# A four-block image kernel on one core: 34 rows in the upper halves of the quads, a tile's weights copied ahead of the hats, the root's table loaded ahead of the evictions of x

## The chip, the cores and the metric

The kernel runs on one core of a Trainium2 chip. The metric is the device time in microseconds; lower is better. The engines are TensorE (PE, with PEld for its weight loads), VectorE (DVE), ScalarE (ACT), GpSimd (POOL) and SyncE, which issues transfers (SP).

## The reference

Four blocks work one after the other on x of shape (2, 32, 64, 64), each as x = x + block(normalised x), where the normalisation is per channel over the pixels of an image:

```python
x = x + _L0_conv_ref(_gn(x), ...)   # deformable 3x3 conv with a mask, batch norm, relu
x = x + _L1_conv_ref(_gn(x), ...)   # 1x1 conv with sign(x) - tanh(x) + tanh(x)
x = x + _L2_conv_ref(_gn(x), ...)   # deformable 3x3 conv: offsets come from a 3x3 conv of x
x = x + _L3_conv_ref(_gn(x), ...)   # attention over the 4096 pixels of an image
```

A deformable convolution first computes, by a plain 3x3 convolution, two offsets for each of nine taps of each pixel; then it samples the image at the shifted positions with bilinear weights (four corners per tap) and convolves the samples.

## The kernel before

Everything is float32 and lives in SBUF. **Quads.** For L0 and again for L2 the normalised image is written four times, as `quads`, once per corner q of the bilinear square, each on its own 32 partitions and shifted by a row or a column, into a grid of rows with a pitch of 66 elements. One write, `quad_write`, handles one corner q, one image b and one half h of the rows, `HALVES`: rows 0 to 32 (33 rows of 64) and rows 33 to 63 (31 rows). Its source is a run of x; its destination is rows of 64 elements at the pitch of 66. VectorE does ten of the sixteen writes (`some_quads`, line 372), ScalarE six (`other_quads`, line 371). TensorE's convolution for the offsets of a half (`offsets_half`, line 1666) waits on the semaphore `quads_ready[b][h]`, for the four corners of the half and of the half above it.

**L0** then turns the offsets (line 1683), makes row weights and samples with matrix products. **L1** ends with its sums in PSUM; VectorE takes their statistics (line 1068), ScalarE copies them to x (`take_sums`, line 1331), and `deviation` (line 1324) takes the square root of the variance on ScalarE, after which VectorE makes scale and bias and both engines write the quads of L2.

**L2.** TensorE's order is written out by hand: the offsets of image 0, their turning (line 1774), the transposes of the quads of image 0 into rows (`rows`, line 1785), the offsets of image 1 and the turned bands, again turning and rows. ScalarE evicts each. VectorE goes from the quads to `corners(0)` (from line 668), `indices(0)`, `place_bands` (ends at line 951, `bands_made`), `corners(1)`, `indices(1)`. SyncE stores the rows to HBM as `quad_table` (line 453), writes the bands' data to HBM once `bands_made` is there (line 459), and reads them back spread over the partitions (line 477): three groups of three taps are asked for in order, the second after the store of the rows of image 1, the third only after three hats.

GpSimd gathers from `quad_table`, nine gathers (one per tap, line 554) for each tile of 128 pixels, into four slots; 53 tiles in all, 21 of image 0 and 32 of image 1. The gather of a tile waits until the tile four before it has been sampled. VectorE weights the corners of a tile (lines 904, 881), adds them (891, 895), TensorE turns the result (1795), ScalarE evicts it and copies the weights of the next tile to PSUM (`tile`, lines 1432 and 1427), TensorE convolves (1803) and VectorE adds to x (919).

The last 11 tiles of image 0 don't use gathers: `dense_and_tiles` runs 27 steps (three stretches of nine taps, of width 384 and then 512) of products with band matrices. In step n VectorE selects bands for step n+1 (`select_bands`, line 966, from the hats across in PSUM), TensorE mixes bands (`mix_bands`, line 1831), VectorE weighs them (line 978) with the hats down, TensorE convolves (line 1841). ScalarE makes the hats: `hats_of_bands(x, y)` makes those across of step x (lines 1456, 1467) and those down of step y (1462, 1471). Tiles of image 0 are worked between the steps, the first beside step 1. Ahead of the steps ScalarE loads a table, makes the hats of steps 0 and 1, waits until both images are indexed, and copies the first tile's weights; VectorE starts `select_bands(0)` only when `first_weights` says that this copy is done.

Eight tiles of image 1 follow, beside the preparation of the attention of image 0; the other 24 tiles of image 1 are merged into the first six of that image's eight blocks of attention; then comes the attention of image 1.

Of the kernel before, what the change touches and what calls it, by code (L numbers as in the profile page):

```python
# [9 lines left out]
ACT = mybir.ActivationFunctionType  # L10
AXIS_X = mybir.AxisListType.X

B, C, H, W = 2, 32, 64, 64
# [53 lines left out]
def build(nc, x, off_w, off_b, conv_w, gamma, beta, l1_w, l1_ax, l1_aw, off2_w, off2_b, conv2_w, conv2_b,  # L67
# [10 lines left out]
    with ctx:  # L78
# [212 lines left out]
        def pair_of(i):  # L291
            return (i, 1, 0)
# [15 lines left out]
        def width(n):  # L308

            return BLK if n >= TAPS else P * (DENSE_TILES - 4 * (DENSE - 1))  # L310
# [38 lines left out]
        def rows_at(value, size=1):  # L349
            return slice(value, value + size) if isinstance(value, int) else bass.ds(value, size)  # L350
# [5 lines left out]

        tile_weights = psum[:, SAMPLES, 3 * P:3 * P + TAPS * CORNERS]

        TOP = H // 2 + 1
        HALVES = ((0, TOP), (TOP, H))  # L360

        def quad_write(op, q, d, b, on_scalar=False, y0=0, y1=H):
# [955 lines left out]
        def _(act):  # L1318
# [7 lines left out]
            def take_sums():  # L1326

                for k in range(NBLK):
                    j = 2 * (k % 4) + k // 4
                    act.wait_ge(block_stat, 2 * NBLK + k + 1)  # L1330
                    act.activation(xs[:, BLK * j:BLK * j + BLK], psum[0:B * C, j, :], ACT.Identity).then_inc(l1_added, 1)
# [93 lines left out]
            def take_weights(n):  # L1425

                return act.activation(tile_weights, corner_w[:, rows_at(n), :].rearrange("p a k -> p (a k)"), ACT.Identity)  # L1427

            def tile(b, pair, u, ahead=True):
                n = tile_no(b, pair, u)  # L1430
                act.wait_ge(turned, lin(n, 1, 1))
                last = act.activation(vals[:, half_of(b, u), :], psum[0:3 * C, SAMPLES, 0:3 * P], ACT.Identity)  # L1432
                if ahead:
                    last = take_weights(lin(n, 1, 1))
                last.then_inc(vals_and_weights, 1)
# [13 lines left out]
            def hats_of_bands(x, y):  # L1449

                if x < STEPS:
                    act.wait_ge(*((bands_loaded[x // 3 % 2], 48 * (x // 6 + 1)) if x else (first_bands, 48)))
                    if x >= 2:
                        act.wait_ge(selected, x - 1)
                    across = psum[:, HATS + x % 2, 0:width(x)]
                    act.activation(across, band_x[x // 3 % 2][:, x % 3, 0:width(x)], ACT.Abs, bias=minus_x[:, :]).then_inc(band_dist_x, 1)
                if 0 <= y < STEPS:
                    act.wait_ge(*((bands_loaded[y // 3 % 2], 48 * (y // 6 + 1)) if y else (first_bands, 48)))
                    if y >= 2:
                        act.wait_ge(band_prods, ROW_SETS * (y - 1))  # L1460
                    for m in range(ROW_SETS):
                        last = act.activation(hat_y[y % 2][:, m, 0:width(y)], band_y[y // 3 % 2][:, y % 3, 0:width(y)], ACT.Abs,  # L1462
                                              bias=band_cols[:, BAND_PAIRS + m:BAND_PAIRS + m + 1])
                    last.then_inc(band_dist_y, 1)
                if x < STEPS:
                    act.wait_ge(band_dist_x, x + 1)
                    act.activation(across, across, ACT.Relu, scale=-1.0, bias=ones[:, 0:1]).then_inc(band_hat_x, 1)
                if 0 <= y < STEPS:
                    act.wait_ge(band_dist_y, y + 1)
                    down = hat_y[y % 2][:, :, 0:width(y)]  # L1470
                    act.activation(down, down, ACT.Relu, scale=-1.0, bias=ones[:, 0:1]).then_inc(band_hat_y, 1)
# [6 lines left out]
            def dense_and_tiles():  # L1478

                act.preload_act_table(ACT.Abs)  # L1480
                act.wait_ge(rows_copied, 9 * B)
                hats_of_bands(0, -1)
                hats_of_bands(1, 0)
                act.wait_ge(indexed, B)
                take_weights(0).then_inc(first_weights, 1)
                for n in range(STEPS):
                    hats_of_bands(n + 2, n + 1)
                    if TILE_AT.get(n - 1) is not None:
                        before = TILE_AT[n - 1]
                        tile(0, pair_of(before // 2), before % 2, ahead=before + 1 < GATHERED[0])  # L1490
                    if n % TAPS == 0 and n:
                        copy_parts(n // TAPS - 1)
                copy_parts(DENSE - 1)
# [10 lines left out]
            def l1_tanh_and_sign(b):  # L1504
                act.wait_ge(l1_g, b + 1)
                if b:
                    act.wait_ge(l1_g_rest, 2)
                act.activation(l1_tanh_q[:, b, :], l1_normed_q[:, b, :], ACT.Tanh, scale=alpha[:, 0:1])
                act.activation(l1_sign_q[:, b, :], l1_normed_q[:, b, :], ACT.Sign).then_inc(l1_tanh, 1)
# [119 lines left out]
            l1_normed()  # L1629
            for b in range(B):  # L1630
                l1_tanh_and_sign(b)
            take_sums()
            act.wait_ge(l1_added, NBLK)
            other_quads(1, lambda: copy_offsets(0, 0))
# [488 lines left out]
```

## Time and profile before

| | |
|---|---|
| median of 3 runs | 1315.96 us (1315.5 to 1316.31) |
| profiled execution: own time | 1317.74 us |
| profiled execution: span of the instructions | 1315.0 us |
| PE busy | 1166.4 us (89%) |
| DVE busy | 1011.4 us (77%) |
| ACT busy | 661.8 us (50%) |
| POOL busy | 484.8 us (37%) |
| mean granted TensorE clock | 0.945 of full speed |

The first row is the time to be changed. The span is that of one profiled execution, from its first instruction to its last; what lies around it is the rest of its own time. A busy share is an average over stages with different limits, so it doesn't say by itself what a change in one stage is worth.

### The profile page before, as it was taken

What the parts mean: (1) busy time and instruction counts of PE and PEld (TensorE: products, weight loads), DVE (VectorE), ACT (ScalarE), POOL (GpSimd) and SP (SyncE); (2) the same over time, 40 slices, a digit from 0 to 9 for tenths busy, and PEclk for the clock granted to TensorE, in tenths of its full rate; (3) what the DMA queues carried; (4) which work ended last, traced back from release to release, by engine and by line L of the source; (5) the groups of instructions that cost most, each with busy time, mean ns of one, the idle gap of its engine ahead of it and who ended that gap; (6) DMA issues with size and microseconds to landing.
All of it is one profiled execution on the core that took longest, in us unless ns stands there. A gap on an engine that the chain in (4) does not pass through costs nothing.

```text
span 1315.0 us, 20260 instructions
## 1 busy us (share of the span) xinstructions
PE 1166.4 (89%) x7066; PEld 490.1 (37%) x7126; DVE 1011.4 (77%) x1679; ACT 661.8 (50%) x882; POOL 484.8 (37%) x537
## 2 busy tenths in 40 slices
PE   4899997586999999978898888888998999999996
PEld 1788884143444443422232322222222222222221
DVE  8799998894766566668879888888766777777772
ACT  4877675644554455322343444444655444444453
POOL 4000000037777777777777777772000000000000
PEclk9999997697999999956799999999999999999999
DMA  2654450048544442111111111110000000000000
GB/s 53 138 131 112 120 103 1 0 127 234 157 124 131 140 151 69 52 47 49 51 54 50 52 51 51 50 50 22 1 1 1 8 9 0 0 0 0 0 1 16
DMA packets 59672, 79.21 MB, mean 60 GB/s; under 512 B 12230, under 2 KB 43974, under 8 KB 59414
## 3 DMA queue, kind: packets, MB, share of 16 engines
q1 hardware_dynamic: 44342, 47.03, 13.6%
q0 software_dynamic: 15264, 31.29, 8.4%
q8 instruction: 43, 0.70, 0.2%
q14 instruction: 23, 0.19, 0.0%
HBM read 70.94 MB, written 7.34 MB: 60 GB/s over the span
## 4 chain that ended last, share of the span: by engine, by line
PE 67%; DVE 21%; issue 5%; ACT 4%; DMA 1%; DVEq 1%; SPq 0%; ACTq 0%; another core or an unknown queue 0%
PE psum L1831 15%; PE psum L1966 12%; PE psum L1948 9%; PE psum L1989 8%; PE psum L1716 6%; DVE maxes L1143 5%; DVE quads L372 3%; PE psum L1731 3%; DVE probs_and_weighted L881 3%; PE psum L1914 3%; PE psum L1743 2%; PE psum L1841 2%; PE psum L1803 2%; PE psum L1995 2%; DVE probs_and_weighted L891 2%
## 5 line engine op out<-in xcount | busy, mean ns | idle before, releaser
L554 POOL DMA_INDIRECT tile_data<-quad_table,index_u x477 | 470.0, 985 | 409.2 <-DMA quad_table<-quad_rows_or_splits 260.7
L1143 DVE TENSOR_REDUCE maxes<-psum 128x1 f32<-128x512 f32 x512 | 329.1, 683 | 98.9 <-PE psum L1948 92.1
L1573 ACT ACTIVATE quads<-psum 128x1024 f32<-128x1024 f32 x256 | 248.1, 1021 | 260.7 <-PE psum L1995 241.5
L1966 PE MATMUL psum<-quads 128*64 128x512 f32 x1024 | 267.0, 616 | 7.1 <-DVE maxes L1143 6.9
L1831 PE MATMUL psum<-scratch,quad_rows_or_splits 128*128 128x512 f32 (+1 forms) x486 | 209.1, 571 | 20.8 <-DVE scratch L966 19.2
L1989 PE MATMUL psum<-quads,probs_and_weighted 32*128 32x512 f32 x1024 | 146.9, 643 | 3.5 <-issue 2.1
L1831 PEld LDWEIGHTS psum<-scratch,quad_rows_or_splits 128*128 128x128 f32 x486 | 87.8, 192 | 117.1 <-issue 101.2
L1948 PE MATMUL psum<-products_or_attention 128*128 128x512 bf16 x226 | 83.8, 414 | 42.6 <-DVE maxes L1143 37.5
L978 DVE TENSOR_TENSOR probs_and_weighted<-psum,quads 128x512 f32<-128x512 f32 (+1 forms) x81 | 51.5, 643 | 79.3 <-PE psum L1831 74.1
L1432 ACT ACTIVATE vals<-psum 96x384 f32<-96x384 f32 x53 | 25.8, 487 | 144.3 <-PE psum L1795 144.3
L1966 PEld LDWEIGHTS psum<-quads 128*64 128x64 f32 x1024 | 55.4, 136 | 107.2 <-issue 100.0
L1716 PE MATMUL psum<-quad_rows_or_splits 64*128 64x128 f32 x1152 | 81.4, 283 | 1.5 <-DVE in_reach L746 1.5
L1948 PE MATMUL psum<-quad_rows_or_splits,tile_data 128*128 128x512 bf16 x226 | 74.4, 387 | 5.5 <-DVE maxes L1143 2.3
L1462 ACT ACTIVATE quads<-quads,band_columns 128x512 f32<-128x512 f32 (+1 forms) x81 | 49.6, 676 | 58.7 <-DVE probs_and_weighted L978 58.7
L1948 PEld LDWEIGHTS psum<-products_or_attention 128*128 (+1 forms) x256 | 20.3, 97 | 153.3 <-DVE maxes L1143 117.0
L1716 PEld LDWEIGHTS psum<-quad_rows_or_splits 64*128 64x128 f32 x1152 | 69.3, 187 | 12.4 <-issue 6.1
L1948 PEld LDWEIGHTS psum<-quad_rows_or_splits,tile_data 128*128 (+1 forms) x256 | 18.0, 96 | 131.5 <-DVE maxes L1143 110.5
L1666 PE MATMUL psum<-quads,off_w 128*32 128x512 f32 x256 | 33.6, 671 | 34.2 <-DVE quads L372 34.2
L966 DVE SCALAR_TENSOR_TENSOR scratch<-products_or_attention,band_columns,psum 128x512 f32<-128x512 f32 (+1 forms) x81 | 51.7, 692 | 12.7 <-ACT psum L1427 12.7
L881 DVE TENSOR_TENSOR probs_and_weighted<-tile_data,psum 128x1152 f32<-128x1152 f32 x45 | 60.6, 1346 | 0.3
L1177 DVE RECIPROCAL scratch<-scratch 32x128 f32<-32x128 f32 x64 | 59.1, 931 | 0.9
L760 DVE TENSOR_TENSOR probs_and_weighted<-psum,tile_data 128x384 f32<-128x384 f32 x96 | 52.8, 549 | 7.0 <-DVE sampled L779 5.1
(226 smaller groups left out, 1431.3 us busy)
## 6 DMA issues: line engine op xcount, KB each, us to landing
products_or_attention<-positions SPq DMA_DIRECT2D x30, 576.0 KB, 8.0
products_or_attention<-bands SPq DMA_DIRECT2D x12, 768.0 KB, 7.6
tile_data<-quad_table,index_u POOLq DMA_INDIRECT x477
quads<-bands SPq DMA_DIRECT2D x6, 768.0 KB, 10.7
quad_table<-quad_rows_or_splits SPq DMA_DIRECT2D x4, 768.0 KB, 9.1
products_or_attention<-bands SPq DMA_DIRECT2D x4, 576.0 KB, 8.4
quad_table<-quad_rows_or_splits SPq DMA_DIRECT2D x2, 640.0 KB, 8.5
products_or_attention<-positions SPq DMA_DIRECT2D x4, 288.0 KB, 6.8
```

What stands on the lines that cost most here:

```text
L554: pool.indirect_dma_start(out=out[:, k * CORNERS * C:(k + 1) * CORNERS * C], out_offset=None, in_=table, in_offset=bass.IndirectOffsetOnAx ...
L760: v.tensor_tensor(out4, psum[:, mix_bank(b, ky), 0:TAP3].rearrange("p (k j c) -> p k j c", k=3, c=C), corner_w[:, rows_at(at), 3 * ROWS4 * ...
L881: v.tensor_tensor(weighted[:, :].rearrange("p (q k c) -> p k q c", q=CORNERS, c=C), corners_of.rearrange("p (k q c) -> p k q c", k=TAPS, q ...
L966: last = v.scalar_tensor_tensor(band_sel[:, n % 2, j, 0:w], band_id[n // 3 % 2][:, n % 3, 0:w], band_cols[:, j:j + 1], psum[:, HATS + n % ...
L1143: v.reduce_max(maxes[:, c // NBLK, c % NBLK:c % NBLK + 1], psum[:, FREE + c % 2, :], AXIS_X)\
L1177: v.reciprocal(inverse[:, part_of], att_sum[C:2 * C, 0, part_of]).then_inc(sum_steps, 1)
L1573: act.activation(probs[:, s % 2, 2 * BLK * h:2 * BLK * (h + 1)], psum[:, SCORES + 2 * h:SCORES + 2 * h + 2, :].rearrange("p a n -> p (a n) ...
L1716: last = pe.matmul(psum[:, mix_bank(b, ky), P * kx:P * kx + P], hat_x[rows, n % 2, 3 * ky + kx, :], img_t[rows, (2 * n + ky) * C:(2 * n + ...
L1831: last = pe.matmul(psum[:, m, 0:width(n)], band_img[:, j, 4 * C * m:4 * C * (m + 1)], band_sel[:, n % 2, j, 0:width(n)], start=j == 0, sto ...
L1948: pe.matmul(psum[:, FREE + c % 2, :], qa[b][:, tile_of_q], ka[b][:, lo:lo + BLK], start=True, stop=True).then_inc(chunk_scored, 1)
L1966: last = pe.matmul(psum[2 * C * h:2 * C * h + 2 * C, SUMS, :], f3[b][:, 4 * s + i, :], probs[:, s % 2, BLK * i:BLK * i + BLK], start=s == ...
L1989: pe.matmul(psum[:, SCORES + i, :], keys[b][mine, P * s:P * s + P], q_now[mine, :], start=True, stop=False)
```

## The change

Three edits. The upper half of a quad write now holds 34 rows and the lower 30. ScalarE copies the first tile's weights as soon as image 0 is indexed, ahead of the hats of steps 0 and 1, instead of after them and after image 1 is indexed. And ScalarE loads the table of the square root after the tanh and sign of L1, ahead of its copies of the sums to x.

```diff
-        TOP = H // 2 + 1
+        TOP = H // 2 + 2
         HALVES = ((0, TOP), (TOP, H))
...
                 act.preload_act_table(ACT.Abs)
                 act.wait_ge(rows_copied, 9 * B)
+                act.wait_ge(indexed, 1)
+                take_weights(0).then_inc(first_weights, 1)
                 hats_of_bands(0, -1)
                 hats_of_bands(1, 0)
-                act.wait_ge(indexed, B)
-                take_weights(0).then_inc(first_weights, 1)
                 for n in range(STEPS):
...
             for b in range(B):
                 l1_tanh_and_sign(b)
+            act.preload_act_table(ACT.Sqrt)
             take_sums()
```

## Rows read from the trace of the kernel before

**Rows 1.** The page's chain that ended last, by engine.

```profile
PE 67%; DVE 21%; issue 5%; ACT 4%; DMA 1%; DVEq 1%; SPq 0%; ACTq 0%; another core or an unknown queue 0%
```

**Rows 2.** Groups by form, DVE: count, busy us and mean ns, idle us before.

```profile
L372 DVE TENSOR_SCALAR quads<-x_state,norm 32x2112 f32<-32x2112 f32 x10 | 24.6, 2462 | 0.3
L372 DVE TENSOR_SCALAR quads<-x_state,norm 32x1984 f32<-32x1984 f32 x10 | 23.3, 2329 | 0.3
...
L1053 DVE TENSOR_SCALAR quad_rows_or_splits<-x_state,norm 32x1024 f32<-32x1024 f32 x6 | 4.8, 802 | 0.1
...
L1085 DVE TENSOR_SCALAR conv_sums_or_normed<-x_state,norm 32x4096 f32<-32x4096 f32 x1 | 2.6, 2578 | 0.0
```

**Rows 3.** Timeline, end of L1 and start of L2: start us, length us, what.

```profile
241.25 4.78 ACT L1331 ACTIVATE x_state<-psum 64x512 f32<-64x512 f32 x8 [4.91 <-DVE stats L1068]
...
246.05 1.28 ACT L1324 ACT_TABLE_LOAD   x1
...
248.05 24.25 DVE L372 TENSOR_SCALAR quads<-x_state,norm 32x2112 f32<-32x2112 f32 x10
...
255.55 6.49 PE L1666 MATMUL psum<-quads,off_w 128*32 128x512 f32 x32 [14.22 <-DVE quads L372]
...
267.13 1.45 PE L1774 MATMUL psum<-ident,scratch 128*128 128x128 f32 x8
...
272.33 0.82 DVE L668 COPY scratch<-psum 128x288 f32<-128x288 f32 x2
```

**Rows 4.** Timeline, from the bands' data to the dense steps 0 to 2.

```profile
286.18 2.63 SPq L459 DMA_DIRECT2D bands<-products_or_attention  x3
...
290.72 1.28 ACT L1480 ACT_TABLE_LOAD   x1
...
296.98 0.58 ACT L1456 ACTIVATE psum<-products_or_attention,minus_x 128x384 f32<-128x384 f32 x1 [4.97 <-DMA quads<-bands]
...
305.15 2.66 SPq L477 DMA_DIRECT2D products_or_attention<-bands  x2
...
306.67 0.18 ACT L1427 ACTIVATE psum<-tile_data 128x36 f32<-128x36 f32 x1
306.96 3.24 DVE L966 SCALAR_TENSOR_TENSOR scratch<-products_or_attention,band_columns,psum 128x384 f32<-128x384 f32 x6 [12.75 <-ACT psum L1427]
...
308.77 9.85 PE L1831 MATMUL psum<-scratch,quad_rows_or_splits 128*128 128x384 f32 x24 [19.19 <-DVE scratch L966]
...
319.21 0.58 ACT L1456 ACTIVATE psum<-products_or_attention,minus_x 128x384 f32<-128x384 f32 x1 [6.75 <-DMA quads<-bands]
...
322.86 0.57 ACT L1456 ACTIVATE psum<-products_or_attention,minus_x 128x384 f32<-128x384 f32 x1
...
328.67 0.49 ACT L1432 ACTIVATE vals<-psum 96x384 f32<-96x384 f32 x1 [1.28 <-PE psum L1795]
...
330.50 0.84 PE L1803 MATMUL psum<-vals,conv_w 96*32 96x128 f32 x6
```

**Rows 5.** Source view of the last load of constants, L424: who waited.

```profile
  PEld psum L1666: 19.0, 1
```

**Rows 6.** Timeline, L0, PE, offsets of image 1's lower half.

```profile
35.80 3.64 PE L1666 MATMUL psum<-quads,off_w 128*32 128x512 f32 x32 [1.01 <-DVE quads L372]
```

**Rows 7.** Waits of POOL's gathers in all: us, times.

```profile
  DVE sampled L895: 4.0, 2
```

**Rows 8.** Timeline: the first gather, the last of tile 28, that tile on DVE.

```profile
281.23 1.59 POOL L554 DMA_INDIRECT tile_data<-quad_table,index_u  x1 [260.70 <-DMA quad_table<-quad_rows_or_splits]
...
621.06 0.94 POOL L554 DMA_INDIRECT tile_data<-quad_table,index_u  x1 [0.30 <-issue]
...
625.40 0.35 DVE L904 CAST index_u<-index_f 128x9 uint32<-128x9 f32 x1
```

**Rows 9.** Timeline, PE, first work after the dense steps.

```profile
568.66 0.87 PE L1795 MATMUL psum<-ident,sampled 128*96 128x128 f32 x3 [4.51 <-DVE sampled L895]
```

**Rows 10.** Stretch: length, PE busy us, granted clock, DMA share, GB/s.

```profile
568.60:616.00 47.40, 41.87 (x111) 0.50 0.16 46
```

## The prediction

> **What bounds the kernel now.** I read the page's chain first. It lies two thirds on PE and one fifth on DVE [rows 1], so a change on ScalarE or in the form of a write pays only where these two stand waiting. Next came the timeline around the three edits. In it the reader is to look at the square brackets, which say how long an engine stood idle and who ended it. Three such places matter. At the start of L2, PE stands idle for 14.22 us until VectorE has written the first quads, while VectorE writes for 24.25 us without a pause, until 272.30 [rows 3]. Ahead of the dense steps, VectorE stands for 12.75 us until ScalarE's copy of the weights, and PE for 19.19 us behind it [rows 4]. And between L1 and L2 a table load of 1.28 us lies between the last copy to x and the root [rows 3]. Last I looked at GpSimd, because work that comes earlier on the other engines can run into it: over all its gathers it waited only 4.0 us for a sampled tile [rows 7], so from 281.23 us on it works at its own pace.
>
> **The table of the root.** ScalarE stands 4.91 us before the first copy of the sums; the load takes 1.28 us there, hidden, and the copies need no table of their own (they follow other tables elsewhere). The last copy ends at 246.03, and the root then starts 1.28 us sooner [rows 3]. The variance is ready before that copy ends, so nothing else is late. Gain 1.3 us; its bounds are 0 (the load is not saved) and 1.3. The Trainium skill (ScalarE: Activation LUTs, What ACT_TABLE_LOAD costs) gives a switch about 2.7 us, load and drain together; by that the sum would be 1.4 us better. The trace disagrees: from the load's end at 247.33 to the first quads at 248.05 there are 0.72 us, which the root and VectorE's scale and bias fill, and no room for a drain.
>
> **34 rows, the price of a write.** VectorE's writes of 2112 and 1984 elements take 2462 and 2329 ns: 133 ns for 128 elements, 1.04 ns each. The same instruction on runs of 1024 and 4096 elements takes 802 and 2578 ns: 0.578 ns each [rows 2]. So one form runs at nearly twice the rate of the other. No row shows 34 or 30 rows. The bounds are 1.04 ns per element (a write of 34 rows takes 2.53 us, of 30 rows 2.26) and 0.578 ns (802 + 1152 x 0.578 = 1468 ns, and 802 + 896 x 0.578 = 1320 ns). I take the fast end: the engine, the operation, the operands and the type are those of the fast rows, and what these have and the slow ones lack is that the written stretch can be cut into two equal parts between rows; 33 and 31 rows can't, 34 and 30 can. The Trainium skill says so outright (VectorE: DVE Perf Modes, Mode 2×_2P — use both read ports for one tensor): two results per cycle where source and destination are in SBUF and the outermost dimension is even. The slow and fast rows agree with it.
>
> Ten writes then take 5 x (1.468 + 1.320) + 10 x 0.03 = 14.2 us instead of 24.25. ScalarE's six writes keep their rate; three grow by one row and three shrink.
>
> **34 rows in L0.** PE's start doesn't move. At 19.0 us it waited for two things, the first quads and the last constants, and the constants' load ends the wait of its weight load [rows 5]. From there PE works without a gap up to the lower half of image 1, where it stood 1.01 us for VectorE's last quads [rows 6]. That wait goes: 1.0 us. PE carries the chain from there.
>
> **34 rows in L2.** Image 0's third write ends after 3 x 1.498 = 4.5 us instead of 7.5: PE starts at 252.5 instead of 255.5, 3.0 us earlier. PE is busy from there to the end of the rows of image 1 almost without a gap, so all its later work comes 3.0 us earlier. VectorE is done with the quads at 262.3, and then waits for the turned offsets. These ended at 267.13 + 1.45 = 268.6 on PE [rows 3], and now end at 265.6. VectorE's copy of the second half thus ends near 266.1 instead of 273.15: 7.0 us earlier. From there it is VectorE alone until `bands_made`, so the store of the bands starts at 279.2 instead of 286.18, and the first bands are there at 290.0 instead of 296.98, the third group's request at 298.1 instead of 305.15 [rows 4]. ScalarE is ready in time: its table load ends at 292.0 - 3.0 = 289.0. Gain on this chain 7.0 us; bounds 3.0 (the transfers turn out to be held by the rows' store) and 7.0. With the slow end of the write's price it is 0, even -0.2 us (three times 0.067 us later for PE).
>
> **The weights ahead of the hats.** I count this in the times of before; the 7 us come off both sides. The copy of 0.18 us [rows 4] falls into ScalarE's wait for the first bands, so it costs nothing. VectorE's first selection then waits only for the hats across of step 0, ready at 298.15 (two operations from 296.98), instead of until 306.96. PE starts at 300.0 instead of 308.77. But only part of these 8.8 us lasts. ScalarE's next hats end at 306.67 as before; steps 0 and 1 run ahead by much of it; then step 3's hats wait for the second group of loads, at 319.21 with or without the edit. From there ScalarE is the chain. Its round of hats takes 3.65 us up to 322.86 and about 3.75 more without the pause of before, to 326.6; the eviction of the first tile follows then, instead of at 328.67. With 0.6 us for its two operations PE convolves that tile at 327.3 instead of 330.50 [rows 4], VectorE goes on with the next tile, and everything behind is 3.2 us earlier. Bounds: 2.0 us (if the granted clock falls in the 4 us in which PE now waits) and 8.8.
>
> **The sum and what takes from it.** 1.0 + 1.3 + 7.0 + 3.2 = 12.5 us for VectorE and PE. GpSimd gains less. Its first gather waited for the rows' store [rows 8] and comes 1.0 + 1.3 + 3.0 = 5.3 us earlier; its two waits of 4.0 us in all fall away but for the usual 0.3 us each: 3.4 us. So from tile 21 on its gathers come 8.7 us earlier, against 12.5 for those who use them. The slack is smallest at tile 28: its last gather was issued by 622.00 and VectorE used it at 625.40 [rows 8], 3.4 us, of which the landing takes a part that the rows don't show. So the gain past tile 28 is capped between 8.7 and 12.1 us; I take 10.5, the middle. Later tiles had more. Against the profiled 1315.0 that is a span of 1304.5. The profiled execution took 1317.74, which is 1.8 us over the median of the runs; I take the gain from the median: 1315.96 - 10.5 = 1305.5 us.
>
> **The rivals.** *No cap*: the landing is short or gathers collide less with VectorE than before; the gain is 12.5, 1303.5 us. For it speaks that one or two microseconds decide; against it that GpSimd waited for hardly anything. *The writes stay slow*: 1.3 + 3.2 = 4.5 us, 1311.5 us; GpSimd's 1.3 + 3.2 (of its 3.4) follow, so no cap. Against it speak the fast rows of the same instruction. *The bands' loads don't follow*: they share the DMA engines with the gathers and the store of rows, and come 3 to 4 us earlier instead of 7; the gain is 8 us, 1308 us. *The clock, the other side*: PE now waits 4 us between steps 2 and 3. After a wait of 4.51 us [rows 9] PE ran at 0.50 of its clock, the lower level of 1.2 GHz, for 47.4 us [rows 10]. If that came in the dense steps, where PE has no gap, it would cost half of 47.4, 23.7 us, less the 10.5: 1329 us. It decides once the clock is down for more than 21 us. Against it: PE was busy for 41.87 of those 47.4 us [rows 10], so there were gaps all along, and the dense steps leave none.
>
> **How the numbers follow.** Forecast with the cap 0.43 (its own range 1304 to 1307.5); no cap 0.20; slow writes 0.15; late loads 0.13; slow writes and hardly anything from the weights, 1314 us, 0.05; clock 0.04. A difference of 0.2%, 2.6 us, is about what a measurement of this kernel can tell from none. All but the last two lie below 1313.3, so faster has 0.91, same 0.05, slower 0.04. The range leaves out the last two and the far end of "no cap": 1302.0 to 1312.0.
>
> **What would show it.** Right: the rows of line 372 near 1.47 and 1.32 us; PE's first matmul of L2 some 5 us earlier in the span (1.0 + 1.3 + 3.0), the first use of bands 9 us earlier, the first tile's convolution 12.5 us earlier; no table load in front of the root; a wait of VectorE's line 904 or a shift of only 9 to 11 us behind tile 28. Wrong: a write of 34 rows at 2.5 us; step 3's hats at 319 less 5 us; a stretch at 0.50 clock in the dense steps.

## The result, and the profile after

| | before | changed kernel | changed kernel, second chip |
|---|---|---|---|
| median | 1315.96 us | 1306.01 us (1302.21 to 1307.63) | 1304.05 us (1302.19 to 1305.9), before there 1314.63 |
| ratio | | 0.9918 [0.9898, 0.9939] | 0.9918 [0.9905, 0.9932] |
| span of the profiled execution | 1315.0 us | 1304.0 us | 1301.9 us |

The change is worth 0.8%, some 10 to 11 us. Lines behind 1632 stand one number higher than before (L1831 is now L1832, and so on).

VectorE's groups by form (count, busy us and mean ns, idle us before) answer to [rows 2]:

```profile
L372 DVE TENSOR_SCALAR quads<-x_state,norm 32x2176 f32<-32x2176 f32 x10 | 14.3, 1429 | 0.3
L372 DVE TENSOR_SCALAR quads<-x_state,norm 32x1920 f32<-32x1920 f32 x10 | 14.1, 1410 | 0.3
```

The twenty writes of the same 64 rows take 28.4 us instead of 47.9. The means mix the two layers. The ten writes of L2 alone (the same view, limited to 244.2 to 258 us) are faster:

```profile
L372 DVE TENSOR_SCALAR quads<-x_state,norm 32x2176 f32<-32x2176 f32 x5 | 7.0, 1403 | 0.2
L372 DVE TENSOR_SCALAR quads<-x_state,norm 32x1920 f32<-32x1920 f32 x5 | 6.3, 1270 | 0.2
```

PE's start in L0, first before, then after (timeline: start us, length us, what; the second block answers to [rows 5, 6]):

```profile
19.00 5.31 PE L1666 MATMUL psum<-quads,off_w 128*32 128x512 f32 x32 [19.00 <-DVE quads L372]
```

```profile
17.76 5.14 PE L1667 MATMUL psum<-quads,off_w 128*32 128x512 f32 x32 [17.76 <-DMA w_sb<-in_b]
...
33.30 3.64 PE L1667 MATMUL psum<-quads,off_w 128*32 128x512 f32 x32
```

PE starts 1.24 us sooner, which I had ruled out, and the wait of 1.01 us is gone. The timeline at the end of L1 and the start of L2 answers to [rows 3]:

```profile
233.86 1.28 ACT L1632 ACT_TABLE_LOAD   x1
238.75 4.78 ACT L1331 ACTIVATE x_state<-psum 64x512 f32<-64x512 f32 x8 [3.61 <-DVE stats L1068]
243.56 0.29 ACT L1324 ACTIVATE mv<-mv,eps 64x1 f32<-64x1 f32 x1
...
244.26 13.66 DVE L372 TENSOR_SCALAR quads<-x_state,norm 32x2176 f32<-32x2176 f32 x10
...
248.59 5.77 PE L1667 MATMUL psum<-quads,off_w 128*32 128x512 f32 x32 [9.77 <-DVE quads L372]
...
259.45 1.45 PE L1775 MATMUL psum<-ident,scratch 128*128 128x128 f32 x8
...
260.94 0.46 DVE L668 COPY scratch<-psum 128x288 f32<-128x288 f32 x1 [0.27 <-PE psum L1775]
```

The root stands right behind the last copy, 0.03 us after its end. The writes take 13.66 instead of 24.25 us. And it is now PE's turn of the offsets that releases VectorE's copy. The dense steps answer to [rows 4]:

```profile
283.04 1.28 ACT L1480 ACT_TABLE_LOAD   x1
284.33 0.20 ACT L1427 ACTIVATE psum<-tile_data 128x36 f32<-128x36 f32 x1
284.58 0.58 ACT L1456 ACTIVATE psum<-products_or_attention,minus_x 128x384 f32<-128x384 f32 x1
285.97 1.66 DVE L966 SCALAR_TENSOR_TENSOR scratch<-products_or_attention,band_columns,psum 128x384 f32<-128x384 f32 x3 [0.31 <-ACT psum L1467]
287.78 11.00 PE L1832 MATMUL psum<-scratch,quad_rows_or_splits 128*128 128x384 f32 x24 [5.88 <-DVE scratch L966]
...
305.87 0.58 ACT L1456 ACTIVATE psum<-products_or_attention,minus_x 128x384 f32<-128x384 f32 x1 [8.20 <-DMA quads<-bands]
...
313.76 0.94 PE L1804 MATMUL psum<-vals,conv_w 96*32 96x128 f32 x6 [3.02 <-ACT psum L1427]
```

The weights' copy lies ahead of the hats. VectorE's wait of 12.75 us is down to 0.31, PE's of 19.19 to 5.88, and in their place stands ScalarE's wait of 8.20 us for the second group of loads (6.75 before). After its 3.02 us without work PE had a mean granted clock of 0.57 for 3.7 us and then 1.00 again (windows; the columns are the length, the busy us of PE, PEld, DVE, ACT and POOL with the number of instructions, the granted clock, the DMA share and GB/s):

```profile
314.60:318.30 3.70, 3.70 (x7) 1.85 (x6) 3.49 (x7) 2.78 (x5) 2.79 (x4) 0.57 1.03 359
318.30:325.00 6.70, 6.66 (x30) 3.68 (x30) 5.78 (x6) 1.08 (x3) 5.01 (x6) 1.00 0.27 77
```

GpSimd's first gather and its last of tile 28, and VectorE's first operation on tiles 27 and 28, answer to [rows 8]:

```profile
273.53 1.13 POOL L554 DMA_INDIRECT tile_data<-quad_table,index_u  x1 [244.24 <-DMA quad_table<-quad_rows_or_splits]
...
610.33 0.95 POOL L554 DMA_INDIRECT tile_data<-quad_table,index_u  x1 [0.30 <-issue]
```
```profile
601.49 0.17 DVE L904 CAST index_u<-index_f 128x9 uint32<-128x9 f32 x1 [2.19 <-DMA tile_data<-quad_table,index_u]
...
612.79 0.24 DVE L904 CAST index_u<-index_f 128x9 uint32<-128x9 f32 x1 [1.51 <-DMA tile_data<-quad_table,index_u]
```

Here the gain shrinks: VectorE waits for two gathers, 3.70 us in all, and none were waited for at these tiles before. The page's chain by engine says the same:

```profile
PE 49%; POOL 19%; DVE 13%; issue 12%; ACT 3%; SPq 1%; DMA 1%; DVEq 1%; POOLq 0%; ACTq 0%
```

PE had 67% of it before [rows 1], and GpSimd does not appear there at all. Followed back from the end, the chain now runs through the gathers. It does so in both profiled executions of the changed kernel (POOL 19% and 18%), and in none of the kernels with one part of the change alone.

**Where the time came from.** I read the same stations in the trace of every kernel of this study: the first of the eight statistics of L1's sums (L1068), the first quads of L2, the store of the bands, and VectorE's first product (L881) of tiles 1, 21, 29 and 30. The distances between them separate the parts of the change, and show what single executions do by themselves (us; each row is one execution, and "own" is the time of that execution):

| kernel | stats at | to quads | to bands' store | to tile 1 | to 21 | to 29 | to 30 | own |
|---|---|---|---|---|---|---|---|---|
| before | 240.53 | 7.52 | 38.13 | 45.53 | 234.28 | 75.24 | 11.27 | 1317.74 |
| before, 8 gathers | 240.68 | 7.51 | 38.35 | 43.74 | 234.27 | 75.58 | 11.28 | 1316.38 |
| table alone | 240.48 | 6.23 | 38.36 | 43.71 | 234.28 | 75.64 | 11.27 | 1311.97 |
| weights alone | 240.63 | 7.51 | 38.36 | 40.50 | 234.59 | 75.63 | 13.14 | 1314.56 |
| 34 rows alone | 239.06 | 7.51 | 30.00 | 45.69 | 234.27 | 75.45 | 13.75 | 1308.04 |
| changed | 238.03 | 6.23 | 30.14 | 40.68 | 234.27 | 78.92 | 13.13 | 1306.74 |
| changed, again | 239.02 | 6.23 | 30.64 | 40.09 | 234.28 | 77.94 | 11.28 | 1303.71 |
| changed, 8 gathers | 239.28 | 6.24 | 30.75 | 42.22 | 234.27 | 75.58 | 11.28 | 1302.84 |

Read down a column, each step shows only where its part of the change is in: 1.3 us for the table, 7.4 to 8.4 us for the rows in L2, 1.2 to 2.6 us for L0. The weights' part is blurred: from the bands' store to tile 1 it takes 43.7 to 45.7 us without them and 40.1 to 42.2 with them. Two columns hold what was lost: 2.4 to 3.7 us between tiles 21 and 29, which goes when a gather is left out, and 0 or about 2 us (1.9 to 2.5) at the first tile of attention, which differs between two executions of one and the same kernel.

### The profile page after: what moved, and what is told of

Same layout as the page of the kernel before. It is cut to its first block, busy times and chain, and to the rows that moved or that the text cites. A ratio compares the mean times of both kernels' runs of the same rounds, so it can differ in the third digit from the quotient of the medians.

```text
span 1304.0 us, 20260 instructions
## 1 busy us (share of the span) xinstructions
PE 1171.8 (90%) x7066; PEld 491.4 (38%) x7126; DVE 993.0 (76%) x1679; ACT 661.4 (51%) x882; POOL 493.6 (38%) x537
## 4 chain that ended last, share of the span: by engine, by line
PE 49%; POOL 19%; DVE 13%; issue 12%; ACT 3%; SPq 1%; DMA 1%; DVEq 1%; POOLq 0%; ACTq 0%
POOL tile_data L554 19%; PE psum L1967 13%; PE psum L1949 8%; PE psum L1990 8%; PE psum L1717 6%; DVE maxes L1143 5%; PE psum L1732 3%; DVE probs_and_weighted L881 3%; PE psum L1744 2%; PE psum L1667 2%; PE psum L1996 2%; DVE probs_and_weighted L891 1%; PE psum L1915 1%; ACT quads L1573 1%; PE psum L1735 1%
## 5 line engine op out<-in xcount | busy, mean ns | idle before, releaser
L554 POOL DMA_INDIRECT tile_data<-quad_table,index_u x477 | 470.0, 985 | 389.3 <-DMA quad_table<-quad_rows_or_splits 244.2
L1832 PE MATMUL psum<-scratch,quad_rows_or_splits 128*128 128x512 f32 (+1 forms) x486 | 211.8, 577 | 5.9 <-DVE scratch L966 5.9
L1832 PEld LDWEIGHTS psum<-scratch,quad_rows_or_splits 128*128 128x128 f32 x486 | 89.1, 194 | 103.7 <-issue 88.7
L1717 PEld LDWEIGHTS psum<-quad_rows_or_splits 64*128 64x128 f32 x1152 | 69.3, 187 | 12.4 <-issue 6.3
L881 DVE TENSOR_TENSOR probs_and_weighted<-tile_data,psum 128x1152 f32<-128x1152 f32 x45 | 60.6, 1346 | 0.3
L1990 PEld LDWEIGHTS psum<-quads,probs_and_weighted 32*128 32x128 f32 x1024 | 40.4, 184 | 47.7 <-issue 37.5
L1667 PE MATMUL psum<-quads,off_w 128*32 128x512 f32 x256 | 32.7, 656 | 27.5 <-DMA w_sb<-in_b 17.8
## 6 DMA issues: line engine op xcount, KB each, us to landing
quads<-bands SPq DMA_DIRECT2D x6, 768.0 KB, 10.8
```

The source lines that it names most:

```text
L554: pool.indirect_dma_start(out=out[:, k * CORNERS * C:(k + 1) * CORNERS * C], out_offset=None, in_=table, in_offset=bass.IndirectOffsetOnAx ...
L881: v.tensor_tensor(weighted[:, :].rearrange("p (q k c) -> p k q c", q=CORNERS, c=C), corners_of.rearrange("p (k q c) -> p k q c", k=TAPS, q ...
L1667: pe.matmul(psum[C * g:C * g + C, bank, :].rearrange("p (y x) -> p y x", x=W), off_w_sb[d][:, s, :], grid[:, y:y + 8, sx:sx + W], start=s ...
L1717: last = pe.matmul(psum[:, mix_bank(b, ky), P * kx:P * kx + P], hat_x[rows, n % 2, 3 * ky + kx, :], img_t[rows, (2 * n + ky) * C:(2 * n + ...
L1832: last = pe.matmul(psum[:, m, 0:width(n)], band_img[:, j, 4 * C * m:4 * C * (m + 1)], band_sel[:, n % 2, j, 0:width(n)], start=j == 0, sto ...
L1990: pe.matmul(psum[:, SCORES + i, :], keys[b][mine, P * s:P * s + P], q_now[mine, :], start=True, stop=False)
```

## The experiments

**Each part by itself.** Three kernels with one part each, and the changed kernel again on that chip, all timed beside the kernel before (1314.63 us there).

```diff
-        TOP = H // 2 + 1                              # 34 rows alone
+        TOP = H // 2 + 2
...
+                act.wait_ge(indexed, 1)               # weights alone
+                take_weights(0).then_inc(first_weights, 1)
                 hats_of_bands(0, -1)
                 hats_of_bands(1, 0)
-                act.wait_ge(indexed, B)
-                take_weights(0).then_inc(first_weights, 1)
...
+            act.preload_act_table(ACT.Sqrt)           # table alone
```

> Only the 34 rows. The stations of the changed kernel say: 2.5 us in L0, 8.0 us more up to the bands' store, so dense steps 10.5 us earlier. Theory, the gathers cap what arrives at tile 28: 10.5 us lies under the cap of this kernel (the first gather comes about 6.4 us earlier, two waits of 3.4 us go, slack 1.8 us: 11.6), so nearly all of it stays: 1305.5 us. Rival, no cap and the parts simply add to the 10 us of the whole: this one alone gives 10 minus 1.3 for the table minus 3.2 to 4.8 for the weights, 1310 to 1311 us.

> Only the weights ahead of the hats. Both theories: the first selection leaves the copy of the weights and waits for the hats of step 0; dense steps 3.2 us earlier once step 3 waits for its loads. The cap is far (the gathers' waits of 3.4 us and the slack of 1.8 us cover it), so 1312.8 us. If it were worth nothing in the end, 1316.0 us, the weights were never on the path that sets the end.

> Only the root's table ahead of the evictions. Theory: the load of 1.28 us hides in ScalarE's idle 4.9 us, everything behind is 1.3 us earlier, 1314.7 us; this is about the size of the measurement's noise, so the trace decides: quads of L2 start 1.28 us earlier. Rival, a switch of tables costs a drain as well: 2.7 us earlier.

> The changed kernel once more, for the spread of its runs: 1302.2 to 1307.6 us in five runs, against 1.4 us for the kernel before. Theory: the time between tile 25 and tile 30 depends on how gathers and VectorE's work meet and on when the granted clock rises after the attention has begun (7.9 us after its first products in the first trace, 3.4 us before the change), so the spread comes back, 1302 to 1308 us, and the trace shows the same first tile of image 1 within 0.5 us and another tile 30. Rival: the spread comes from the start (L0, L2), and then the first tile of image 1 moves as well.

Measured:

| kernel | median us | ratio to before |
|---|---|---|
| 34 rows alone | 1306.16 | 0.9927 [0.9911, 0.9944] |
| weights alone | 1312.58 | 0.9980 [0.9972, 0.9989] |
| table alone | 1314.09 | 0.9993 [0.9981, 1.0004] |
| changed kernel again | 1304.05 | 0.9918 [0.9905, 0.9932] |

By the ratios the parts add up to 1.00% (0.73 + 0.20 + 0.07), 13.1 us, and the whole gives 0.82%, 10.8 us. The difference of 2.4 us is smaller than the uncertainty of these four ratios taken together (some 3.4 us, an estimate from their intervals), so that something is lost in coming together is read from the traces and not from these times. The 34 rows alone gave 9.6 us (7.4 to 11.7), which leaves out the rival's 5 to 6: in front of the tiles they were 8.0 to 9.5 us ahead, and VectorE waited for no gather in this kernel. The table's 1.3 us can be seen in its trace (6.23 instead of 7.51 us) but not in its time, whose interval holds 1. The weights' own trace shows their part at work, where before 12.75 and 19.19 us stood:

```profile
290.81 0.20 ACT L1427 ACTIVATE psum<-tile_data 128x36 f32<-128x36 f32 x1
...
296.82 1.66 DVE L966 SCALAR_TENSOR_TENSOR scratch<-products_or_attention,band_columns,psum 128x384 f32<-128x384 f32 x3 [2.30 <-ACT psum L1467]
298.64 10.54 PE L1831 MATMUL psum<-scratch,quad_rows_or_splits 128*128 128x384 f32 x24 [10.26 <-DVE scratch L966]
...
317.24 0.58 ACT L1456 ACTIVATE psum<-products_or_attention,minus_x 128x384 f32<-128x384 f32 x1 [8.75 <-DMA quads<-bands]
```

PE's first step is 10.1 us earlier, step 3's hats only 2.0 us: most of the lead ends in the wait for the second group of loads, as the prediction had it. When these loads land differs by itself: step 3's hats come 31.0 to 34.0 us behind the bands' store in the four kernels of the table without the weights' edit and 30.7 to 32.6 in the four with it. Counted from step 3's hats the edit shows clearly: tile 1 follows after 11.6 to 12.7 us without it and 9.1 to 9.8 with it, 2.8 us on average.

The changed kernel's second execution answers the question after the spread only in part: tile 30 stands 1.9 us apart in its two traces (641.40 and 639.48), as the theory said, but the first tile of image 1 (tile 21) moved as well, by 0.9 us the other way (549.35 and 550.26), where the theory allowed 0.5.

**One gather of nine left out.** If GpSimd is what takes part of the gain, the cap must go with less work for it. From the fifth tile of L2 on, both kernels leave out the ninth gather of a tile, so the ninth tap uses the samples of an earlier tile.

```diff
-            def gather(table, out, rows, done):
-                for k in range(TAPS):
+            def gather(table, out, rows, done, taps=TAPS):
+                for k in range(taps):
...
-                            gather(quad_table[1][b], gathered[:, slot, :], slot, gathers[slot])
+                            gather(quad_table[1][b], gathered[:, slot, :], slot, gathers[slot], TAPS - 1)
...
-                v.wait_ge(gathers[slot], lin(turn, 16 * TAPS, 16 * TAPS))
+                v.wait_ge(gathers[slot], lin(turn, 16 * (TAPS - 1), 16 * TAPS))
```

> The kernel before, with eight instead of nine gathers a tile from the fifth tile of layer 2 on (the ninth tap takes the samples that an earlier tile left in its slot), so GpSimd's tile falls from about 11.2 to about 10.0 us and its margin at tile 28 grows from 3.5 us to over 25. Theory (GpSimd's gathers did not bound the kernel before, they only stood close): the time stays within 1.5 us of the kernel before, about 1314. Rival (the gathers already bounded it): clearly faster, by 3 us or more.

> The changed kernel with the same eight gathers. Theory (the gain of 16.6 us in front of the tiles is capped by the gathers at tiles 27 and 28, which took 4.1 us): VectorE waits for no gather, its start of tile 28 stands 16 to 17 us ahead of that of the kernel before, and the time is 4 us under the changed kernel's, about 1300.5 if the start of attention keeps its clock. Rival (the gain shrinks for another reason, as the clock at the start of attention, and the waits for gathers are only a sign): 1303 to 1306, as the changed kernel.

Measured: before with 8 gathers 1316.32 us, 1.0008 [0.9997, 1.0020] of the kernel before; the changed kernel with 8 gathers 1302.95 us, 0.9911 [0.9896, 0.9927]. The first is what the theory said, and not the rival's 3 us or more: the gathers did not bound the kernel before. The margin at tile 28 is 11.5 us instead of 3.4, not the 25 expected, because GpSimd now waits for sampled tiles. In the second VectorE waits for no gather at all, the chain of its page has no GpSimd in it, and the way from tile 21 to 29 is 75.58 us as in the kernels before, instead of 78.9 and 77.9. So the stretch that was lost is the gathers'. The time came out 2.5 us above the 1300.5 of the theory, and 1.1 below the changed kernel's on the chip before it: the intervals of the two overlap, and the time alone would not have decided it. With eight gathers in both kernels the change is worth 0.97%, 12.8 us, with nine 0.82%, 10.8 us: the way of the theory, but within the noise. In this execution the bands' loads landed later (tile 1 came 42.22 us after their store, against 40.1 and 40.7), so only 11.8 us of gain stood in front of the tiles, and all of it was left at tile 28 (612.60 against 624.39) and at tile 30.

**An earlier start of the tiles.** The other side of the same question: give VectorE and PE a lead that GpSimd does not share. The store of image 1's rows, three transfers that take about 10 us on the queue together, is issued behind step 1's loads of bands.

```diff
                 if m == 1:
-                    store_rows(1)
                     sp.wait_ge(indexed, B)
                     sp.wait_ge(rows_turned, 9 * B)
+                if m == 2:
+                    store_rows(1)
```

> The changed kernel with the three transfers that store image 1's rows issued one step later, behind step 1's loads of bands on the queue instead of ahead of them. Both theories: ScalarE's 8.20 us wait for the loads of step 1 shrinks by 4 to 6 us, and tile 0 starts about 5 us earlier. Theory of the cap: GpSimd is not touched, tile 28 and the end stand where they stood, the time stays within 1 us of the changed kernel (1304 to 1306). Rival (the dense steps set the end): 4 to 5 us faster, about 1300.

Measured: 1302.91 us (1300.2 to 1304.32), 0.9906 [0.9890, 0.9921]. ScalarE's wait of 8.20 us is gone altogether and tile 1 stands 36.64 us behind the bands' store, against 40.1 to 40.7: a lead of 3 to 4 us, less than the 5 I expected. What became of it, in VectorE's timeline (lines of this kernel are one higher):

```profile
578.44 0.17 DVE L905 CAST index_u<-index_f 128x9 uint32<-128x9 f32 x1 [1.36 <-DMA tile_data<-quad_table,index_u]
...
589.81 0.18 DVE L905 CAST index_u<-index_f 128x9 uint32<-128x9 f32 x1 [2.77 <-DMA tile_data<-quad_table,index_u]
...
602.22 0.17 DVE L905 CAST index_u<-index_f 128x9 uint32<-128x9 f32 x1 [2.62 <-DMA tile_data<-quad_table,index_u]
...
613.62 0.17 DVE L905 CAST index_u<-index_f 128x9 uint32<-128x9 f32 x1 [1.61 <-DMA tile_data<-quad_table,index_u]
```

Four waits of 8.36 us in all instead of two of 3.70, and tile 28 stands at 613.70, where the changed kernel has 612.94 and 612.74. Tile 21 was 2.0 and 2.9 us ahead of those two executions, tile 28 is 0.8 and 1.0 behind them, about as GpSimd, which started 1.8 and 0.5 us later. This is the clearest reading of the cap: at tile 28 nothing of the lead is left. The time is less clear. It lies 1 us under the 1304 to 1306 that the theory expected and 3 above the rival's 1300; by the ratios it is 1.6 us below the changed kernel's, with intervals that overlap.

**Work moved into the waits.** If the gathers fix when tile 28 starts, work of VectorE that stands behind it can go ahead of it for nothing.

```diff
-SCORED_BESIDE = [0, 0, 0, 4, 8, 8, 12, 0]
+SCORED_BESIDE = [0, 0, 0, 4, 12, 8, 8, 0]     # maxima ahead
+SCORED_BESIDE = [0, 0, 0, 8, 12, 12, 0, 0]    # all ahead
```

> The changed kernel with four of attention's score maxima moved from beside tile 6 of the last group of tiles to beside tile 4, so ahead of the two waits for gathers (2.19 and 1.51 us at tiles 27 and 28). Theory of the cap: VectorE works in the time that it waited, the wait at tile 27 shrinks to nothing or nearly, the rest of the tiles is shorter by what was moved, and the time falls by about 3 us, to 1302. Rival (the waits only shift to the next tile, since GpSimd's gathers stay where they are): the sum of waits stays 3 to 4 us and the time does not move.

> Both earlier edits at once: image 1's rows are stored a step later, and four maxima stand beside tile 4 instead of tile 6. Alone the late store brought 8.4 us of waits for gathers at tiles 24 to 28 and about 1 us in the time. Theory (GpSimd's gathers fix the start of tile 28 at about 613.7 us, and work moved ahead of it is done in the waits): tile 28 stands where it stood, tile 29 starts 2.9 us sooner after it, and the time is 2 to 3 us under that of the late store alone, about 1300.5. Rival (VectorE's order is not what bounds the last tiles): no change, about 1303.

> The late store with all maxima beside tiles 3 to 5 (8, 12 and 12 of them) and none beside tile 6. Theory (as before, with 12 instead of 4 maxima moved ahead of tile 28; 8.4 us of waits hold about 12 maxima): tile 28 still starts at 613.7 us, tile 29 is bounded by its gather (624.9), about 4 us ahead of the late store alone, and the time is 1299. Rival (the maxima don't fit into the waits and push tile 28 later): 1303 or above.

| kernel | median us | ratio to before | tile 28 at | to 29 | to 30 | own |
|---|---|---|---|---|---|---|
| changed, again | 1304.05 | 0.9918 [0.9905, 0.9932] | 612.74 | 15.46 | 11.28 | 1303.71 |
| maxima ahead | 1304.43 | 0.9917 [0.9902, 0.9931] | 613.80 | 12.56 | 12.96 | 1305.31 |
| late store | 1302.91 | 0.9906 [0.9890, 0.9921] | 613.70 | 15.34 | 13.84 | 1304.32 |
| late store, maxima ahead | 1301.49 | 0.9901 [0.9885, 0.9917] | 610.01 | 12.71 | 11.27 | 1297.71 |
| late store, all ahead | 1302.53 | 0.9897 [0.9881, 0.9914] | 616.30 | 9.05 | 11.33 | 1303.91 |

The traces follow the theory: the four maxima leave 12.56 us between tiles 28 and 29 instead of 15.46, and the one wait that is left is 0.45 us. In the kernel with the late store the two above 0.2 us up to tile 28 are these (a third of 0.73 us comes at tile 33):

```profile
587.20 0.17 DVE L905 CAST index_u<-index_f 128x9 uint32<-128x9 f32 x1 [1.55 <-DMA tile_data<-quad_table,index_u]
...
609.90 0.20 DVE L905 CAST index_u<-index_f 128x9 uint32<-128x9 f32 x1 [0.30 <-DMA tile_data<-quad_table,index_u]
```

The times don't follow as far. The maxima alone brought nothing (1304.43 where I expected 1302), with the late store 1.4 us more than the late store alone by the medians, of different chips, and 0.7 by the ratios. Tile 28 did not stay where it was either: it came at 610.01, 3.7 us sooner than with the late store alone, and GpSimd's first gather was 2.2 us sooner there for reasons ahead of this edit. With all twelve ahead theory and rival were each half right: tile 29 did wait for its gather (0.54 us, at 625.16), but the maxima no longer fit into the waits, and tile 28 came at 616.30 instead of 613.7. "Late store, maxima ahead" has the lowest median of all kernels here and "late store, all ahead" the lowest ratio, but both intervals overlap the changed kernel's; that they are faster, by some 2 us, is not shown.

**The number of rows.** Is it the even number that makes the write fast, or something of the 34?

```diff
-        TOP = H // 2 + 2
+        TOP = H // 2 + 3    # 35 and 29 rows
+        TOP = H // 2 + 4    # 36 and 28 rows
```

> The changed kernel with 35 and 29 rows in the halves of the quads instead of 34 and 30 (2240 and 1856 elements a row, again even numbers, but odd numbers of rows). Theory (VectorE's fast write needs an even number of rows in the outer dimension): each write falls back to the slow pace, 2.5 and 2.1 us, the quads of layer 2 take 22 to 24 us instead of 13.66, and most of the gain is gone: 1310 to 1313. Rival (33 rows were slow for their size or their address, and any larger half is fast): 1.46 us a write, and the time of the changed kernel.

> The changed kernel with 36 and 28 rows. Theory (an even number of rows is what counts): 1.50 us for the write of 2304 elements and 1.23 for that of 1792, the quads in layer 2 take about 13.7 us, and the time is that of the changed kernel within 1 us. Rival (34 rows are a special size): slow writes of 2.6 us and 1311 or more.

VectorE's groups by form, first of the kernel with 35 rows, then of that with 36:

```profile
L372 DVE TENSOR_SCALAR quads<-x_state,norm 32x2240 f32<-32x2240 f32 x10 | 26.0, 2596 | 0.3
L372 DVE TENSOR_SCALAR quads<-x_state,norm 32x1856 f32<-32x1856 f32 x10 | 22.0, 2196 | 0.3
```
```profile
L372 DVE TENSOR_SCALAR quads<-x_state,norm 32x2304 f32<-32x2304 f32 x10 | 14.9, 1491 | 0.3
L372 DVE TENSOR_SCALAR quads<-x_state,norm 32x1792 f32<-32x1792 f32 x10 | 13.4, 1343 | 0.3
```

One row more makes the write 1.8 times as long, two rows more make it fast again. The times are 1311.63 us (0.9973 [0.9960, 0.9987]) and 1306.05 us (0.9934 [0.9912, 0.9955]): with 35 rows the table and the weights alone are left, 0.27%, which is what they gave by themselves (0.20 + 0.07). The theory holds, with two misses in its numbers: the write of 1792 elements was expected at 1.23 us and took 1.34 on average (1.20 in L2), and the time with 36 rows is the changed kernel's only within the noise (0.9934 against 0.9918).

## Why the prediction was right

The forecast was 1305.5 us, measured were 1306.01 and 1304.05, and the mechanism was the predicted one: 34 rows at the fast rate, the weights ahead, the table hidden, and a cap by GpSimd's gathers at the end of the tiles. The number was met with some luck: more gain stood in front of the tiles than predicted, and more of it was taken, and the two errors cancel. Where the sum was off is the same each time, a term too small: L0's, that of the rows in L2, and what the gathers take. By its steps:

**The price of a write.** Predicted 1468 and 1320 ns, ten writes 14.2 us. Measured 1403 and 1270 ns and 13.66 us in L2, and 1429 and 1410 over both layers. Between 30 and 34 rows L2 gives 0.52 ns per element, half of the slow form's 1.04; the 0.578 of the rows used was a little high. The experiment with 35 and 36 rows shows what was only argued: an even number of rows is fast and an odd one slow. The Trainium skill (VectorE: DVE Perf Modes, Mode 2×_2P) asks for an outermost dimension that is even, or odd and equal in source and destination; the traces agree, 2596 ns at 35 rows and 1491 at 36. Whether the odd ones would be fast with a source that the engine takes as 35 rows too, no run shows.

What the prediction left out is GpSimd. In L0, three of VectorE's ten fast writes are longer than in L2 (1.62, 2.33 and 1.53 us in the changed kernel), and GpSimd's setting of constants beside them takes longer too. One of these operations in GpSimd's timeline, before and after:

```profile
16.24 0.21 POOL L538 MEMSET ones<- 128x128 f32 x1
```
```profile
21.37 1.32 POOL L538 MEMSET ones<- 128x128 f32 x1
```

Both are so in all nine traces with 34 or 36 rows and in none of the five with 33 or 35, so the fast write and GpSimd's work hold each other up; by what, no run tests. In L2 GpSimd has nothing to do during the writes, and there each of them has its full pace.

**L0, 1.0 us: mis-sized, and its reason failed.** "PE's start doesn't move" is the step. With 33 rows PE started at 18.95 to 19.09 in every trace and with 35 at 19.46, released by the quads; with 34 or 36 at 17.76 to 17.78, released by the constants. So the constants had landed at 17.8, and it was VectorE's third quads that held PE until 19.0; the source view's row for the weight load [rows 5] named the constants for a wait that two semaphores had to end, while the matmul's own bracket named the quads. L0 gives 1.2 us for the start and 0 to 1.0 for the wait behind it (1.01, 0.61, 0.52 us and none in the four traces with 33 rows), and PE's first 32 matmuls take 5.0 to 6.5 us from execution to execution, with the edit and without. So L1's statistics come 1.2 to 2.6 us sooner over the traces of the table above, 1.5 in the middle.

**The table, 1.3 us.** 7.51 us became 6.23. The Trainium skill (ScalarE: Activation LUTs, What ACT_TABLE_LOAD costs) has about 2.7 us for a switch; here 1.28 us was all there was to save, both as the load's length and as the gain.

**L2, 7.0 us.** Measured 7.4 to 8.4. PE's start came 3.17 us earlier within L2 instead of 3.0; what is beyond is PE's first 32 matmuls, 5.77 us long instead of 6.49, since the clock rose sooner in them (a mean granted clock of 0.62 instead of 0.55; 5.19 to 6.49 us over the traces of this study, without a link to the edit). The rest is as predicted: VectorE's copy is released by PE's turn of the offsets and everything up to the bands' store moves with it. The rival of late loads fell: the hats of step 0 come 12.4 us sooner in the span, those of step 3 13.3.

**The weights, 3.2 us.** Measured 2.8 on average over eight traces, from step 3's hats to tile 1; the time of the edit alone gives 2.6 us (1.4 to 3.7). The pair of first profiles gives 4.8 us from the bands' store to tile 1 (45.53 and 40.68), but of the four kernels without this edit two took 43.7 us there and two 45.5 and 45.7. A difference between two single traces holds such things.

**The cap, 2.0 us taken from 12.5.** Right in place and kind, too small in both numbers. In front of the tiles stood 13.6 us or so (1.5 + 1.3 + 8.0 + 2.8), 16.6 in the pair of first profiles. VectorE's waits for gathers then took 3.7 and 2.6 us. At tile 28 VectorE stood 12.5 us earlier than before (612.94 against 625.48, 11.4 against the trace with eight gathers), where the prediction had taken 10.5 as the middle of 8.7 to 12.1; in the first execution the slow start of attention then took another 1.9, so that the span came out 11.0 us shorter. The cap itself was 10.7 us for GpSimd's last gather of tile 28 (622.00 to 611.28) where I had 8.7: its start gained 7.7 us instead of 5.3 (2.5 + 1.3 in front of the quads of L2 and 3.9 behind them, where I had 1.0 + 1.3 + 3.0), and its two waits of 4.0 us went as predicted. And of the slack of 3.4 us the landing takes 1.5 to 2.7 us, which stand between the end of the last gather and VectorE's use in the eight places of three traces (both of the changed kernel, and the late store) where it was waited for (611.28 to 612.79 above). The rival without a cap, 1303.5 us, is out: its waits are there, in both profiles, and they grow with the lead.

**The clock.** The rival was that PE falls to the lower clock in the dense steps. It did, after the 3.02 us in which it had no work, but for 3.7 us, not for 21 or more. PE also works longer at the lower level at the very start of these steps, for 6.1 us (287.80 to 293.90, mean clock 0.50) against 3.8 before (308.77 to 312.60, 0.51), and its first 24 matmuls take 11.00 us instead of 9.85; the prediction had not looked there either. Where it cost something I had not looked: at the first tile of attention, when PE is busy nearly all the time (5.99 of 7.00 us below) and still has 0.5 of its clock. Below are three windows in order: the changed kernel's first execution, its second, and before (columns as in the windows above).

```profile
628.30:635.30 7.00, 5.99 (x30) 1.70 (x24) 4.45 (x6) 3.65 (x5) 5.32 (x6) 0.51 0.20 56
```
```profile
628.20:631.30 3.10, 2.47 (x14) 0.30 (x6) 3.03 (x4) 2.56 (x3) 2.36 (x3) 0.65 0.21 54
```
```profile
641.20:643.80 2.60, 2.27 (x13) 0.30 (x6) 2.52 (x5) 2.06 (x2) 1.99 (x3) 0.53 0.21 61
```

By the mean clocks of these windows PE keeps the lower of its two levels, 1.2 GHz, for some 7, 2.2 and 2.5 us from the start of tile 29, and the tile takes 13.13, 11.28 and 11.27 us. Five of twelve executions of kernels with nine gathers have the long form (12.96 to 13.84 us), with the edits and without (13.14 for the weights alone), and in these five the lower level lasts 6.8 to 8.9 us into the tile, in the other seven 1.1 to 2.5. Since one kernel has both, it is nothing that the edits set; the runs of the changed kernel spread over 5 us, and this is one piece of it. What decides it stays open, and so does why the times of "maxima ahead" stayed where they were while its waits went: its profiled execution had the long form (12.96 us), but five timed runs can't be explained by one profile.

## What to carry to other kernels

A cap by an engine off the critical path is seen best by its margins: list, tile by tile, when the data was issued and when it was used, and compare the smallest margin with the expected gain before counting the gain. A single pair of traces can be off by 2 us at places that no edit touches; the distance between fixed stations over several traces, the one-part kernels among them, tells the edit from the execution. Where a write is cut in two for another engine's sake, cut it so that both parts have an even number of rows, and look at what GpSimd does beside the faster write.

## What the runs showed that was not expected

- VectorE's write has two paces: 2461 ns for 33 rows, 1403 for 34, 2595 for 35, 1469 for 36, all in L2, of one operation on the same 32 partitions. Times in between (1.53 and 1.62 us) stand only in L0, beside GpSimd's work.
- A wait for two semaphores can be shown at the weight load as that for the one and at the matmul as that for the other (19.0 us: the constants in the one view, the quads in the other). The matmul's bracket was the right one here.
- The first tile of attention takes 11.3 us or about 2 more in executions of the same program, by how long PE stays at half its clock.
- GpSimd's indirect transfers take 0.94 us with 0.30 between them, and some of them up to 2.6 us; in the changed kernel the first went out 7.7 us sooner, and 29 tiles of nine took 337.8 us where they had taken 340.8 with 4.0 us of waits.
